# In the last three groups of attention, TensorE weighs the values of two steps together in every odd step

## What is computed

```
h = modulate(rmsnorm(x, g1), scale_msa, shift_msa)
q, k, v = split(h @ Wqkv.T + bqkv)              # 16 heads of 32
q = rmsnorm(q, gq) * 32 ** -0.5 ; k = rmsnorm(k, gk)
o = softmax(q @ k.T) @ v
x = x + gate_msa * (o @ Wproj.T + bproj)
h = modulate(rmsnorm(x, g2), scale_mlp, shift_mlp)
x = x + gate_mlp * (gelu(h @ Wfc1.T + bfc1) @ Wfc2.T + bfc2)
```

## Time and profile before

| | |
|---|---|
| median of three runs | 1768.58 us |
| the profiled execution | 1769.43 us |
| its span | 1767.6 us |
| TensorE busy | 1720.9 us (97%) |
| VectorE busy | 1054.2 us (60%) |
| ScalarE busy | 976.1 us (55%) |
| granted TensorE clock, mean | 0.996 |

### The profile page before, as it was taken

The page is one execution under the profiler, slowest core; times in us unless marked ns, Lnnn a source line. Parts: engine busy times, 40 slices in busy tenths (PEclk is TensorE's granted clock), DMA queues, the critical chain, the costliest instruction groups (busy, mean ns, idle before and its releaser), DMA issues.

```text
span 1767.6 us, 23560 instructions
## 1 busy us (share of the span) xinstructions
PE 1720.9 (97%) x8476; PEld 1151.0 (65%) x8476; DVE 1054.2 (60%) x1269; ACT 976.1 (55%) x1272; POOL 391.5 (22%) x303
## 2 busy tenths in 40 slices
PE   8999999999999999999998999999999999999999
PEld 5655555555555555554334878888888888888887
DVE  6678887889998899888777454142322324142301
ACT  4577777798888889889886432222222212221221
POOL 3001110111111111000150233333333333333332
PEclk9999999999999999999999999999999999999999
DMA  8554554555565555556765202010020202010000
GB/s 289 130 156 127 144 145 114 136 150 143 143 160 127 152 143 132 150 138 158 179 144 209 60 18 66 19 54 24 18 65 6 65 18 65 18 53 24 18 18 24
DMA packets 122245, 176.96 MB, mean 100 GB/s; under 512 B 29568, under 2 KB 43904, under 8 KB 121136
## 3 DMA queue, kind: packets, MB, share of 16 engines
q1 hardware_dynamic: 119648, 163.75, 34.8%
q10 hardware_dynamic: 1712, 9.47, 1.4%
q0 software_dynamic: 800, 2.62, 0.5%
HBM read 124.87 MB, written 50.92 MB: 99 GB/s over the span
## 4 chain that ended last, share of the span: by engine, by line
PE 79%; DVE 11%; ACT 5%; issue 3%; DMA 1%; SPq 1%; ACTq 0%; POOL 0%; DVEq 0%
PE scores L1470 20%; PE scores L564 10%; PE pv L1487 10%; PE gemm L1487 10%; PE pv L581 9%; PE gemm L660 7%; DVE sums L895 7%; PE pv L1442 4%; PE gemm L673 4%; ACT probs L808 4%; PE aux L598 2%; DVE raw L920 1%; DMA wstage<-in_wqkvT 1%; PE aux L1457 1%; PE aux L612 1%
## 5 line engine op out<-in xcount | busy, mean ns | idle before, releaser
L808 ACT ACTIVATE probs<-scores,shift 128x1024 f32<-128x1024 f32 x512 | 550.5, 1114 | 125.7 <-PE scores L564 116.7
L895 DVE TENSOR_TENSOR sums<-sums,probs 128x2048 f32<-128x2048 f32 x186 | 439.1, 2361 | 26.9 <-ACT probs L808 24.0
L564 PE MATMUL scores<-q_stack,k_stack 128*128 128x512 f32 x1024 | 348.9, 425 | 9.5 <-ACT probs L808 7.9
L1470 PE MATMUL scores<-w_hi,act_parts 128*128 128x512 f32 x1016 | 316.3, 393 | 0.0
L564 PEld LDWEIGHTS scores<-q_stack,k_stack 128*128 128x128 f32 x1024 | 172.1, 188 | 196.1 <-ACT probs L808 90.8
L1402 POOL TENSOR_TENSOR act_parts<-act_full,act_parts 128x512 fp32r<-128x512 f32 x127 | 169.7, 1336 | 478.6 <-ACT act_parts L1333 478.6
L581 PE MATMUL pv<-probs,v 128*32 128x512 f32 x2048 | 257.8, 601 | 0.4 <-ACT probs L808 0.4
L1470 PEld LDWEIGHTS scores<-w_hi,act_parts 128*128 128x128 f32 x1016 | 189.9, 189 | 38.7
L1333 ACT ACTIVATE act_parts<-act_full 128x512 fp32r<-128x512 f32 x127 | 80.3, 632 | 221.3 <-PE scores L1470 220.4
L1470 PE MATMUL scores<-w_lo,act_parts 128*128 128x512 f32 x508 | 198.4, 391 | 0.0
L1546 DVE TENSOR_TENSOR y_next<-pv,p_bias 128x512 f32<-128x512 f32 x28 | 19.3, 691 | 299.7 <-PE pv L1442 299.7
(11 more groups left out here) (197 smaller groups left out, 2062.2 us busy)
## 6 DMA issues: line engine op xcount, KB each, us to landing
k_stack<-parts_scratch SPq DMA_DIRECT2D x128, 256.0 KB, 4.9
q_stack<-parts_scratch SPq DMA_DIRECT2D x128, 256.0 KB, 5.4
parts_scratch<-parts SPq DMA_DIRECT2D x62, 512.0 KB, 3.1
inverse<-inverse_scratch SPq DMA_DIRECT2D x128, 64.0 KB, 2.1
heads_out<-o_out SPq DMA_DIRECT2D x32, 256.0 KB, 4.5
out<-result SPq DMA_DIRECT2D x30, 256.0 KB, 2.0
heads<-heads_out SPq DMA_DIRECT2D x28, 256.0 KB, 4.0
x_tile<-in_x SPq DMA_DIRECT2D x28, 256.0 KB, 2.8
```

The lines of the kernel that those rows point to most:

```text
L564: mm = nc.tensor.matmul(scores[p][:, i, :], k_stack[s][:, h, j * P:(j + 1) * P], q_stack[half][:, h, :], start=True, stop=True)
L808: nc.scalar.activation(probs[L % RING][:, 2 * p:2 * p + 2, :], scores[p][:], ACT.Exp, bias=small["shift"][:]).then_inc(exp_done, 1)
L895: nc.vector.tensor_tensor(sums[:], a[:], probs[l % RING][:], ALU.add).then_inc(added, 1)
L1470: mm = nc.tensor.matmul(acc[t], parts_of(c, m)[:, b, t * P:(t + 1) * P], w2[a][:, m, :], start=(m == 0 and i == 0), stop=(m == NM - 1 and ...
```

## The change

`PAIRED` becomes `AFTER`, which is 256. So all steps through 255 weigh in pairs: an even step from 208 on weighs nothing, and an odd one weighs L - 2 and L - 1. The sums of rows, in odd steps too, keep their place behind `qk(L, 1)` and ahead of the weighing.

```
-PAIRED = max(FILL)
+PAIRED = AFTER
```

## The result

| | before | after |
|---|---|---|
| median, same chip | 1769.12 us (4 runs) | 1787.24 us (4 runs) |
| profiled execution | 1769.43 us | 1787.31 us |
| its span | 1767.6 us | 1785.5 us |
| TensorE busy | 1720.9 us | 1718.7 us |

The ratio is 1.0101, 95% interval 1.0088 to 1.0114: the change costs about 18 us. The forecast was 1785.6 us, in a range of 1778.5 to 1790.

A forecast was written before the change was run, and what follows sets the result against it. The prediction took a loop of TensorE-ScalarE hand-overs as the bound. Terms 2.05 + 13.0 + 1.7 + 0.2 = 17.0 us on the profiled 1769.43 gave 1786.4; the median, 0.85 lower, 1785.6, range 1778.5 to 1790.

The forecast's parts named there:

- The chain of hand-overs: Late attention steps: a loop between TensorE and ScalarE, 4.68 us for two steps, sets the time; forecast given 0.83.
- The predicted pair: Two ordinary steps: the second weighing delays the next even step's first scores, adding 0.86 us to 4.68.
- the start: Steps 208 to 217: partly hidden by ScalarE's other work, so step 218 comes 2.05 us later.
- The four halves: Steps 218 to 250, in four stretches of eight steps: each takes 23.89 us, together +13.0 us.
- The slow additions of the third half: VectorE's four additions of up to 3.19 us, which lengthened that half by 0.77, fit within the longer pairs.
- a thin cover: At the start: if step 210 or 212 is not hidden, up to 0.9 us more.
- The end: Steps 250 to the projection: two ordinary pairs +1.7 us, and three weighings behind the last scores +0.2.
- The first rival: TensorE's own work is the bound and fewer changes of shape shorten it: 8.9 us faster, about 1760; chance 0.04.
- VectorE: Second rival: its additions set the pace at 4.70 us for two steps, so no change, 1768 to 1770; chance 0.03.
- ScalarE's waits for its sums: In the profile after, exponentials no longer wait for VectorE's sums; before, the prediction cited one such wait, at 866.93.
- the rival of a falling clock: TensorE idle some 1.9 us per 5.54 us pair drops its clock: 78 us more, about 1864; chance 0.03.
- The lower bound: First weighing begins once two scores are issued, 0.27 us less per pair: 6.5 less, 1779; as third rival, chance 0.07.

The follow-up runs named there:

- the half-way version: The change in the first 24 of the 48 steps alone (`PAIRED` = 231), against the kernel before: 1778.53 against 1769.79 us, 1.0053.
- the first experiment: The changed kernel with its six pairs with sums of rows weighed one step at a time again: 1782.63 us against 1770.04 for the kernel before, 1.0070.
- the last variant: The kernel before, with sums of rows alone in row steps 217 to 249 and two weighings in the next even step: 1768.87 against 1770.03 us, 0.9993.

## Why the prediction was right

The chain of hand-overs was the bound, and one piece of it grew by 0.86. The predicted pair (5.54) was measured as 5.55 in the changed kernel. The forecast of 1785.6 was 1.6 us short of the median: 0.3 of it is the start, below, and the rest is of the size of the scatter ahead of step 207, which no part of the argument covers. The two halves of the argument are shown apart: the place in the queue by the extra weighing (14.8 us in odd steps, 0 in even ones) and by the scores moved between the weighings; the sum of 24 pairs by the half-way version (8.7 of 18).

Point by point:

- *The four halves.* 13.0 predicted, 12.96 measured. The slow additions of the third half were hidden, as worked out.
- *The start.* 2.05 predicted, 2.4 measured. Step 210 was hidden. Step 212 was not: it waited 0.23 for scores, and with TensorE later from there step 214 started 0.65 late (843.16, less the 0.7 of scatter, against 841.81) instead of 0.32. The text had named this as what a thin cover would cost.
- *The end.* 1.9 predicted, 2.0 measured.
- *Less than TensorE's own work.* The first rival (faster by fewer changes of shape) fell with the extra work in even steps. Its mechanism exists and was worth 2.8 us, over 10 pairs, in steps 176 to 207, where TensorE is the bound.
- *VectorE.* It was not the pace of the changed kernel. The prediction said that ScalarE's waits for its sums vanish. The page shows five of 1.83 us under VectorE's name, but by the code and by the first experiment they are waits for scores, so what was said holds. Before the change VectorE was nearer to being the limit than the prediction's reading had it: the exponentials waited for additions not once but four times between 836 and 950 us, 2.4 us in all.
- *The clock* stayed at 1.00 with about 1.1 us of idle time in each 5.5 us pair in front of scores (0.82 and 0.27; the prediction had counted 1.9), so the rival of a falling clock fell. Of the rule on short idle times between groups ("TensorE: Matmul & The Clock Gate" of the Trainium skill, section "A second HAM failure mode: psum-queue depth-cycling") nothing was seen here.
- *The lower bound* (the first weighing 0.27 earlier) was not needed: 858.13 + 0.73 = 858.86 is where it begins.

## What to carry to other kernels

When two engines hand work to each other, ask what stands in the queue ahead of the instruction that the other waits for, not how much work there is in all: the same weighing cost 0.86 us in one place and nothing in the next. Putting two pieces of work together pays where their engine is the bound and loses where a hand-over behind them is. When the profile names a releaser, read in the code what the instruction waits for before believing or dismissing it: here VectorE was named five times where no wait for it stood, and a load was named once that was the true one.

## What was not expected of the hardware

- A load of keys that took 11.10 us to land in the last variant, against 9.5 at most before, and held TensorE up for 0.98 us at 878.33. It was seen once, and why it was slower is open.
- Pairing where TensorE is full brought 0.28 us a pair (1.2 to 4.6 us over 10 pairs), and single rows (0.99 against 0.86 for a weighing, 0.68 against 0.44 for scores) said 0.35 to 0.37.
